# A Mamba-2 block on one core: the order of two matmul groups in TensorE's queue

## The chip, the core and the metric

The kernel runs on one core of a Trainium2 chip. The time is that of the device for one launch, in microseconds. A core has TensorE (matmuls), VectorE, ScalarE, GpSimd and SyncE, each with an instruction queue of its own that is worked off in order; they meet at semaphores. TensorE writes to PSUM only, eight banks of 128 partitions by 512 float32.

## The reference

Input x is 4 batches of 512 tokens by 512 features. All is float32.

```
mod = silu(c) @ wmod                              # shift, scale, gate for both halves
h   = layernorm(x) * (1 + ca) + sa
xBC, z, A_log = split(h @ in_proj_w.T)            # 2048, 1024 and 64 columns
xBC = silu(causal depthwise conv1d(xBC, 4 taps) + bias)
X, B, C = split(xBC)                              # 64 heads of 16; B and C: 8 groups of 64
dt  = softplus(A_log)
y   = chunked state space scan(X, -dt, B, C) + D * X / dt
x   = x + ga * ((y * silu(z + z_bias)) @ out_proj_w.T)
h   = layernorm(x) * (1 + cb) + sb
x   = x + gb * (h @ binarize(w_ffn).T + b_ffn)
```

The scan, for each head and each chunk of tokens, is the sum of a diagonal part, (C B^T masked by the decays inside the chunk) times X, and an off-diagonal part, C times the state that the chunks before have left, scaled by the decay. The state of a chunk is B^T times X weighted by the decay to the chunk's end.

## The kernel before

There are three parts: a first one (layer norm, modulation, weights split in a high and a low half), the main part (input projection, convolution, scan), and a tail (output projection, second layer norm, the last linear layer). The change is in the main part.

The main part goes over 16 steps, a step being one of four pairs of B/C groups (16 heads) and one of four batches. A step has four units of 128 tokens (`U_TOK`), two chunks of 64 each. That makes `NU` = 64 units. The loop runs `v` from -2 to 63, with four slots `sl` in each turn, and every engine has a copy of this loop with its own order of calls. In one turn TensorE runs for unit `v` the scan's matmuls, and prepares later ones:

- slot 0: `offdiagonal(v)` (L1241), `states(v + 1)` (L1254), `gram(v + 1)` (L1280), `diagonal(v)` (L1266);
- slot 1: `turn_x(v + 2)` (transposes of X, L1218);
- slots 2 and 3: `decay(v + 2, 0)` and `(v + 2, 1)` (L1209), and in slot 3 `turn_b(v + 2)` (L1227);
- in nearly all slots `project` (L1200), half a tile of the input projection: 6 matmuls of 128*128 by 512 columns; in some turns `weights` (L1297), two transposes of the next weights; and at the end matmuls of the tail (L1968).

`gram` makes C B^T of a unit, four matmuls of 64 rows by 64 columns of the array (64*64), into columns 384 to 447 of the two PSUM banks named `pair` (`YS`). `diagonal` is 32 matmuls of 64*32, into columns 0 to 127 of the same banks. `offdiagonal` (64*64, columns 128 to 255) and `states` (64*64, columns 256 to 383) write there too. In the trace each of these float32 matmuls has two records: 8 for `gram`, 64 for `diagonal`, 16 for `offdiagonal`, 8 for `states` (half of these two in some units). A matmul that is marked as the last of a group raises the group's semaphore: `g_done`, `yd_done`, `yo_done`, `st_done`.

Other engines on these groups:

- ScalarE writes the exponentials M of a unit (`exponent`, L1373, slots 2 and 3, waits for `yd_done` two units back), X transposed (`spread`, L1381), B transposed (`copy_b`, L1386, raises `bt_read`).
- VectorE, slot 1: `update(v + 1, 0)` adds a chunk's state (L1514, L1517), after `st_done`, `yd_done` and `g_done`; `collect(v)` reads `offdiagonal` and `diagonal` (L1500, L1502), after `yd_done`, `yo_done` and `g_done` of the next unit. Slot 2: `update(v + 1, 1)`, then `mix(v + 1, q)` (L1484) multiplies M by gram's result, after `exp_done` and `g_done`, and raises `m_done`, two for each unit. Convolution taps (L1454) and silu products (L1475) fill the queue between.
- GpSimd weighs X by the decays (`weigh`, L1587), fades the state (L1597), and builds the gated output (L1608, L1622); L1629 makes the low halves of weights.

Of the kernel before, what the change touches and what calls it, by code (L numbers as in the profile page):

```python
# [58 lines left out]
def wait(eng, sem, count):  # L59

    if not isinstance(count, int) or count > 0:
        eng.wait_ge(sem, count)
# [886 lines left out]
def piece_at(slot):  # L949

    gp, r = slot // 64, slot % 64
    if r == 0 and gp > 0:
        return (gp - 1) * 12 + 11
    if r in W_AT and gp < GP - 1:
        return gp * 12 + W_AT[r]
    j = (slot - 4 * OUT_UNIT - 3) // 4 * 2 + (slot % 4 == 0)
    if slot >= 4 * OUT_UNIT + 3 and slot % 4 in (3, 0) and j < NWO + NWF:
        return NWP + j
    return None
# [7 lines left out]
def main_part(nc, s, outer, start, x, w_in, w_out, w_ffn, b_ffn):  # L967

    with ExitStack() as ctx:
# [3 lines left out]
        def sem(name):  # L973
            return outer.enter_context(nc.semaphore("m_" + name))
# [22 lines left out]
        d_done, exp_done, xt_done, xp_done, xw_done, bt_done, bt_read, g_done, m_done = (  # L997
            sem(n) for n in ("d_done", "exp_done", "xt_done", "xp_done", "xw_done", "bt_done", "bt_read", "g_done", "m_done"))
# [16 lines left out]
        def chunk(u, c):  # L1015
            first = (u % UPS) * U_TOK + c * Q
            return slice(first, first + Q)
# [26 lines left out]
        def n_new(u, c):  # L1044

            return (u // UPS) * (NC - 1) + min(2 * (u % UPS) + c + 1, NC - 1)
# [135 lines left out]
        def tensor(pe, tail):  # L1182
            def project(k, part):

                n, t = TILES[k]
                if part == 0:
                    if n % NB == 0 and n >= NB:

                        pe.wait_ge(w_lo_done, (n // NB - 1) * 12 + 2 * W_ORDER.index(t) + 2)
                    if n < NB:  # L1190

                        pe.wait_ge(start.w_pool, start.weights_ready(t))
                        start.wait_low(pe, 4 * n + 3)
                    if k < 3:
                        pe.wait_ge(start.h_act, 5 + k)
                        pe.wait_ge(start.w_act, (4, 8, 12)[k])
                    wait(pe, silu_done, k - 2)
                for m in range(6 * part, 6 * part + 6):
                    kc, w, h = m // 3, (s.w_hi, s.w_hi, s.w_lo)[m % 3], (s.h_hi, s.h_lo, s.h_hi)[m % 3]
                    ins = pe.matmul(A[k % 3][:, :], w[:, t, kc, :], h[:, n % NB, kc, :], start=(m == 0), stop=(m == 11))  # L1200
                if part == 1:
                    ins.then_inc(in_done, 1)

            def decay(u, q):

                if q == 0:
                    pe.wait_ge(rl_ready[u % 2], 64 * (u // 2 + 1))
                wait(pe, exp_done, 2 * u + q)
                pe.matmul(DB[:, :], s.Lm[:, u % 2, q, :], s.R[:, u % 2, q, :], start=True, stop=True).then_inc(d_done, 1)  # L1209
# [11 lines left out]
            def turn_b(u):  # L1221

                n = u // UPS
                if u % UPS == 0:
                    pe.wait_ge(silu_done, TILE_NO[n, 2] + 1)
                wait(pe, bt_read, u)
                pe.transpose(GB[:, 0:P], Bt[:, n % 2, tok(u)], s.ident[:, :]).then_inc(bt_done, 1)  # L1227

            def offdiagonal(u):

                n = u // UPS
                wait(pe, y1_done, u)
                pe.wait_ge(s_new, n_new(u, 1))
                pe.wait_ge(m_done, 2 * u + 2)
                for c in range(2):
                    if u % UPS == 0 and c == 0:
                        continue
                    for j in range(2):
                        for q in range(2):
                            group, strip = slice(64 * q, 64 * q + 64), slice(64 * j, 64 * j + 64)  # L1240
                            ins = pe.matmul(YS[strip, q, P + Q * c:P + Q * c + Q], S[group, (2 * u + c - 1) % 4, strip],  # L1241
                                            Ct[group, n % 2, chunk(u, c)], start=True, stop=True)
                ins.then_inc(yo_done, 1)

            def states(u):

                if u > 0:
                    pe.wait_ge(s_new, n_new(u - 1, 1))
                pe.wait_ge(xw_done, u + 1)
                pe.wait_ge(bt_read, u + 1)  # L1250
                for q in range(2):
                    for c in range(2 if u % UPS < UPS - 1 else 1):
                        half, group = slice(64 * c, 64 * c + 64), slice(64 * q, 64 * q + 64)
                        ins = pe.matmul(YS[group, c, 256:384], BTs[half, group], Xw[half, q, :], start=True, stop=True)  # L1254
                ins.then_inc(st_done, 1)

            def diagonal(u):

                pe.wait_ge(m_done, 2 * u + 2)
                pe.wait_ge(xp_done, u + 1)  # L1260
                for q in range(2):
                    for e in range(2):
                        for j in range(4):
                            for c in range(2):
                                half, h = slice(64 * c, 64 * c + 64), 2 * j + e
                                ins = pe.matmul(YS[32 * j:32 * j + 32, c, q * Q:(q + 1) * Q], Xp[half, u % 2, HG * q + h, :],  # L1266
                                                M[half, u % 2, q, h * Q:(h + 1) * Q], start=(e == 0), stop=(e == 1))
                ins.then_inc(yd_done, 1)

            def gram(u):  # L1270

                n = u // UPS
                if u % UPS == 0:
                    pe.wait_ge(silu_done, TILE_NO[n, 3] + 1)
                pe.wait_ge(bt_read, u + 1)
                wait(pe, m_done, 2 * u)
                for c in range(2):
                    for q in range(2):
                        group = slice(64 * q, 64 * q + 64)
                        ins = pe.matmul(YS[64 * c:64 * c + 64, q, 384:384 + Q], Bt[group, n % 2, chunk(u, c)],  # L1280
                                        Ct[group, n % 2, chunk(u, c)], start=True, stop=True)
                ins.then_inc(g_done, 1)
# [26 lines left out]
            for v in range(-2, NU):  # L1309
                u = v + 2  # L1310
                for sl in range(4):
                    slot = 4 * v + sl
                    if (v, sl) == (-2, 2):
                        start.turn_sections(pe)
                    if (v, sl) == (-1, 0):
                        start.dt_inputs(pe, 1, 1)
                        start.gate_turn(pe)
                    if sl == 0:
                        if v >= 0:
                            offdiagonal(v)  # L1320
                        if 0 <= v + 1 < NU:
                            states(v + 1)
                        if 0 <= v + 1 < NU:
                            gram(v + 1)
                        if v >= 0:
                            diagonal(v)
                    if sl == 2 and u < NU:
                        decay(u, 0)
                    if sl == 3 and u < NU:
                        decay(u, 1)  # L1330
                    if slot + 8 in PART_AT:
                        project(*PART_AT[slot + 8])
                    if sl == 1 and u < NU:
                        if slot >= 1 and piece_at(slot - 1) is not None:
                            pe.wait_ge(w_copied, piece_at(slot - 1) + 1)
                        if v in (-2, 5):
                            pe.wait_ge(start.we_ev, UPS if v < 0 else 2 * UPS)
                        turn_x(u)
                    if sl == 3 and u < NU:
                        turn_b(u)  # L1340
                    if v >= 0 and piece_at(slot) is not None:
                        if sl == 3:
                            pe.wait_ge(xp_done, u + 1)
                        weights(piece_at(slot))
                    if (v, sl) == (4, 3):
                        pe.wait_ge(xp_done, u + 1)
                        start.end_turn(pe, 1)
                    if slot in TAIL_AT:
                        tail.project(pe, *TAIL_AT[slot])
                    if (v, sl) == (NU - 1, 1):  # L1350
                        alpha()
# [696 lines left out]
```

## Time and profile before

| | |
|---|---|
| median of 3 runs | 698.25 us (697.37 to 699.26) |
| the profiled execution | 698.25 us, its span 696.5 us |
| TensorE clock granted, mean | 0.966 of full |
| matmuls / weight loads busy | 637.1 / 499.8 us |
| VectorE / ScalarE / GpSimd busy | 519.6 / 383.4 / 356.2 us |

The span is the time from the first to the last instruction in the trace. "PE" is TensorE's matmuls, "PEld" its weight loads, "DVE" VectorE, "ACT" ScalarE, "POOL" GpSimd, "SP" SyncE; L1280 is line 1280 of the kernel. Matmuls are pipelined: one record lasts longer than the distance to the next start, so distances between starts tell more than durations. A tile shape such as 64*32 is the rows and columns of the array that a matmul uses. A "q" behind an engine's name means its sequencer.

### The profile page before, as it was taken

How to read it: one execution, taken by the hardware profiler on the slowest of the kernel's cores; microseconds unless marked ns; L12 is line 12 of the kernel's file. 1: busy time of each engine (PE TensorE's matmuls, PEld its weight loads, DVE VectorE, ACT ScalarE, POOL GpSimd, SP SyncE). 2: the span in 40 equal slices, each digit the busy share in tenths (PEclk: the TensorE clock that was granted, in tenths of full speed). 3: DMA queues.
4: the chain of work that ended last, by engine and by line, in shares of the span. 5: the costliest groups of instructions: out<-in, count | busy, mean ns of one | idle time of the engine just before them, and what ended most of it. 6: DMA issues, size and time to landing. Idle time of an engine off the chain costs nothing.

```text
span 696.5 us, 21359 instructions
## 1 busy us (share of the span) xinstructions
PE 637.1 (91%) x8371; PEld 499.8 (72%) x8371; DVE 519.6 (75%) x947; ACT 383.4 (55%) x834; POOL 356.2 (51%) x416
## 2 busy tenths in 40 slices
PE   4576987999999999999999999999997899999995
PEld 1463665777777777777777777878775667888884
DVE  6559749997787787867778678777779556786766
ACT  3647532554655545564645565555665525666555
POOL 4546310244754634655445375363754747667652
PEclk9679878999999999999999999999999999999999
DMA  8644202052322222232123142422212664354411
GB/s 280 158 147 136 80 4 75 11 165 76 111 64 87 68 66 70 75 118 69 36 82 111 40 140 83 142 79 74 81 51 81 207 208 122 121 145 145 135 46 61
DMA packets 61914, 70.52 MB, mean 101 GB/s; under 512 B 13972, under 2 KB 33460, under 8 KB 61816
## 3 DMA queue, kind: packets, MB, share of 16 engines
q1 hardware_dynamic: 61816, 69.17, 31.4%
q8 instruction: 67, 1.10, 0.7%
q14 instruction: 31, 0.25, 0.1%
HBM read 54.45 MB, written 14.70 MB: 99 GB/s over the span
## 4 chain that ended last, share of the span: by engine, by line
PE 71%; DVE 13%; issue 5%; POOL 4%; ACT 4%; DMA 1%; SPq 0%; DVEq 0%; POOLq 0%; ACTq 0%
PE bank L1200 32%; PE bank L1968 11%; PE pair L1266 6%; PE bank L1209 4%; PE bank L2001 3%; PE pair L1254 3%; DVE m_cv L1454 2%; PE pair L1241 2%; PE bank L1297 2%; PE bank L1218 2%; DVE chain L600 2%; DVE m_M L1484 1%; PE pair L769 1%; DVE chain L593 1%; DMA h_lo_place<-y_scratch 1%
## 5 line engine op out<-in xcount | busy, mean ns | idle before, releaser
L1454 DVE SCALAR_TENSOR_TENSOR m_cv<-bank,gpc,m_cv 128x511 f32<-128x511 f32 (+2 forms) x192 | 143.3, 747 | 35.5 <-ACT m_cv L1361 30.9
L1200 PE MATMUL bank<-h_hi,w_hi 128*128 128x512 f32 x384 | 160.4, 418 | 2.9 <-POOL h_lo L428 1.5
L1200 PE MATMUL bank<-h_lo,w_hi 128*128 128x512 f32 x384 | 153.0, 399 | 0.0
L1200 PE MATMUL bank<-h_hi,w_lo 128*128 128x512 f32 x384 | 153.0, 398 | 0.0
L1597 POOL TENSOR_TENSOR m_S<-m_S,m_cd 128x128 f32<-128x128 f32 x96 | 39.9, 415 | 160.8 <-DVE m_S L1517 85.4
L1361 ACT ACTIVATE m_cv<-bank,gpc 128x512 f32<-128x512 f32 x96 | 72.0, 750 | 76.7 <-PE bank L1200 75.7
L1200 PEld LDWEIGHTS bank<-h_hi,w_hi 128*128 128x128 f32 x384 | 74.1, 193 | 21.3 <-issue 4.7
L1200 PEld LDWEIGHTS bank<-h_hi,w_lo 128*128 128x128 f32 x384 | 73.4, 191 | 16.9
L1200 PEld LDWEIGHTS bank<-h_lo,w_hi 128*128 128x128 f32 x384 | 74.0, 193 | 14.1
L1373 ACT ACTIVATE m_M<-bank 128x512 f32<-128x512 f32 x128 | 76.2, 595 | 12.7 <-PE bank L1209 11.2
L1484 DVE TENSOR_TENSOR m_M<-m_M,pair 128x512 f32<-128x512 f32 x128 | 81.7, 679 | 0.2 <-issue 0.2
L1587 POOL TENSOR_TENSOR m_Xw<-m_Xp,wend 128x256 f32<-128x256 f32 x64 | 39.9, 623 | 73.8 <-ACT m_Xp L1381 73.8
L1368 ACT ACTIVATE bank<-m_cv 128x512 f32<-128x512 f32 x96 | 58.1, 605 | 3.4 <-DVE m_cv L1454 3.4
L1209 PE MATMUL bank<-R,Lm 84*128 84x512 f32 x128 | 58.2, 454 | 1.8 <-ACT m_M L1373 1.8
L1822 POOL TENSOR_TENSOR t_y_lo<-h_lo_place,t_y_hi 128x1024 fp32r<-128x1024 f32 x16 | 39.1, 2444 | 39.6 <-ACT t_y_hi L1768 35.1
L1266 PE MATMUL pair<-m_M,m_Xp 64*32 64x64 f32 x4096 | 55.5, 225 | 0.2 <-issue 0.2
L1475 DVE SCALAR_TENSOR_TENSOR m_gate<-bank,m_cv 128x512 f32<-128x512 f32 x32 | 22.1, 690 | 42.1 <-ACT bank L1368 42.1
L1968 PE MATMUL bank<-h_hi,t_y_hi 128*128 128x512 f32 x128 | 51.5, 403 | 1.3 <-POOL t_y_lo L1822 1.3
L1968 PE MATMUL bank<-h_hi,t_y_lo 128*128 128x512 f32 x128 | 50.7, 396 | 0.0
L1968 PE MATMUL bank<-h_lo,t_y_hi 128*128 128x512 f32 x128 | 50.7, 396 | 0.0
L1381 ACT ACTIVATE m_Xp<-bank 128x256 f32<-128x256 f32 x64 | 24.3, 380 | 46.3 <-PE bank L1218 46.3
L1266 PEld LDWEIGHTS pair<-m_M,m_Xp 64*32 64x32 f32 x4096 | 44.9, 106 | 4.7 <-issue 0.3
(184 smaller groups left out, 1280.9 us busy)
## 6 DMA issues: line engine op xcount, KB each, us to landing
m_ea<-ea_scratch SPq DMA_DIRECT2D x32, 256.0 KB
m_dd<-dd_scratch SPq DMA_DIRECT2D x32, 256.0 KB
y_scratch<-m_t SPq DMA_DIRECT2D x16, 512.0 KB, 3.5
h_lo_place<-y_scratch SPq DMA_DIRECT2D x16, 512.0 KB, 4.4
p_wm<-in_L_wmod_dram SPq DMA_DIRECT2D x6, 1024.0 KB, 7.5
m_wraw<-in_L_attn_in_proj_w_dram SPq DMA_DIRECT2D x18, 256.0 KB, 3.1
w_lo_place<-in_L_attn_input__dram SPq DMA_DIRECT2D x16, 256.0 KB, 4.7
out_dram<-t_o SPq DMA_DIRECT2D x16, 256.0 KB, 2.3
```

Of the source, the lines that this page charges most:

```text
L1200: ins = pe.matmul(A[k % 3][:, :], w[:, t, kc, :], h[:, n % NB, kc, :], start=(m == 0), stop=(m == 11))
L1209: pe.matmul(DB[:, :], s.Lm[:, u % 2, q, :], s.R[:, u % 2, q, :], start=True, stop=True).then_inc(d_done, 1)
L1266: ins = pe.matmul(YS[32 * j:32 * j + 32, c, q * Q:(q + 1) * Q], Xp[half, u % 2, HG * q + h, :], M[half, u % 2, q, h * Q:(h + 1) * Q], star ...
L1361: act.activation(cv[:, k % 3, :], A[k % 3][:, :], ACT.Identity, scale=scale, bias=bias).then_inc(lin_done, 1)
L1368: act.activation(A[k % 3][:, :], cv[:, k % 3, :], ACT.Tanh).then_inc(tanh_done, 1)
L1373: act.activation(M[:, u % 2, q, :], DB[:, :], ACT.Exp).then_inc(exp_done, 1)
L1454: ins = dve.scalar_tensor_tensor(out=cv[:, k % 3, lag:], in0=A[k % 3][:, 0:L - lag], scalar=s.gpc[:, gp, o:o + 1], in1=cv[:, k % 3, lag:], ...
L1484: dve.tensor_tensor(m, m, g, ALU.mult).then_inc(m_done, 1)
L1587: pool.tensor_tensor(Xw[:, :, :].rearrange("p q (j e d) -> p (q j) e d", e=2, d=HD), src, w, ALU.mult).then_inc(xw_done, 1)
L1597: pool.tensor_tensor(S1[:, c, :].rearrange("p (h d) -> p h d", h=HG), S[:, (m - 1) % 4, :].rearrange("p (h d) -> p h d", h=HG), cd[:, b // ...
L1822: pool.tensor_tensor(y_lo[:, st.b % 2, :, :], yt_v(st.b), y_hi[:, st.b % 2, :, :].bitcast(F32), ALU.subtract).then_inc(ylo_done, 1)
L1968: ins = pe.matmul(OB[i][:, :], y[:, i, k, :], w[k], start=(k == 0 and m == 0), stop=(k == KI - 1 and m == 2))
```

## The change

In `gram` a wait goes: the one on `m_done` for count 2u. In TensorE's loop, slot 0, `diagonal(v)` moves from behind `gram(v + 1)` to before it. TensorE's order in slot 0 becomes `offdiagonal(v)`, `states(v + 1)`, `diagonal(v)`, `gram(v + 1)`. The waits of the other engines stay as they are.

```diff
@@ -1273,7 +1273,6 @@
                 if u % UPS == 0:
                     pe.wait_ge(silu_done, TILE_NO[n, 3] + 1)
                 pe.wait_ge(bt_read, u + 1)
-                wait(pe, m_done, 2 * u)
                 for c in range(2):
                     for q in range(2):
                         group = slice(64 * q, 64 * q + 64)
@@ -1320,10 +1319,10 @@
                             offdiagonal(v)
                         if 0 <= v + 1 < NU:
                             states(v + 1)
+                        if v >= 0:
+                            diagonal(v)
                         if 0 <= v + 1 < NU:
                             gram(v + 1)
-                        if v >= 0:
-                            diagonal(v)
                     if sl == 2 and u < NU:
                         decay(u, 0)
                     if sl == 3 and u < NU:
```

## Rows read from the trace of the kernel before

**Rows 1.** Busy us, share of the span and instructions of each engine.
```profile
PE 637.1 (91%) x8371; PEld 499.8 (72%) x8371; DVE 519.6 (75%) x947; ACT 383.4 (55%) x834; POOL 356.2 (51%) x416
```

**Rows 2.** Busy us of each engine by stretch (start:end, length), then clock, DMA share, GB/s.
```profile
100.00:136.00 36.00, 30.22 (x437) 23.38 (x438) 34.57 (x57) 15.56 (x32) 6.98 (x12) 0.86 0.13 43
...
157.00:507.00 350.00, 346.41 (x5865) 275.04 (x5868) 268.09 (x516) 197.52 (x434) 181.54 (x239) 1.00 0.26 83
507.00:551.00 44.00, 36.94 (x643) 28.48 (x630) 34.95 (x72) 25.68 (x60) 27.64 (x35) 0.96 0.35 110
```

**Rows 3.** The chain of waits by line, 157 to 507 us, then 507 to 551.
```profile
by line: PE bank L1200 56.3%; PE pair L1266 10.5%; PE bank L1209 6.3%; PE pair L1254 5.3%; PE pair L1241 4.2%; PE bank L1297 3.4%; PE bank L1218 2.9%; issue 2.1%; PE pair L1280 1.7%; PE bank L1227 1.5%; DVE m_cv L1454 1.3%; POOL m_t L1622 1
...
by line: PE bank L1200 24.4%; DMA h_lo_place<-y_scratch 15.5%; issue 11.7%; DVE m_cv L1454 6.9%; DVE m_M L1484 4.4%; PE bank L1209 3.4%; PE bank L1297 2.9%; DVE t_wsta L1523 2.8%; DVE t_att L1528 2.8%; SPq L1080 2.6%; DVE m_S L1517 2.0%; PE
```

**Rows 4.** The chain in order of time, pieces of L1266: start us, length us.
```profile
135.67 0.79 PE pair L1266 x53
...
558.31 0.79 PE pair L1266 x53
```

**Rows 5.** Gram's matmuls, 157 to 507 us: ns min/median/max, first and last start.
```profile
L1280 PE MATMUL pair<-m_Ct,m_Bt x400: 216/218/267, 157.4 to 506.3; 64*64 64x64 f32 x134
```

**Rows 6.** Groups by line, whole span: busy us, mean ns, idle before.
```profile
L1280 PE MATMUL pair<-m_Ct,m_Bt 64*64 64x64 f32 x512 | 22.6, 223 | 0.0
```

**Rows 7.** Semaphore instructions of the wait helper on TensorE, 200 to 500 us.
```profile
L62 PEldq EVENT_SEMAPHORE  x157: 51/51/51, 200.4 to 498.9; - x157
```

**Rows 8.** TensorE matmuls in order, 305.9 to 308.5 us: start us, length us.
```profile
306.09 0.38 PE L1297 MATMUL bank<-ident,m_wraw 128*128 128x128 f32 x2
306.40 0.46 PE L1241 MATMUL pair<-m_Ct,m_S 64*64 64x64 f32 x16
306.71 0.45 PE L1254 MATMUL pair<-m_Xw,m_BTs 64*64 64x128 f32 x8
306.95 0.32 PE L1280 MATMUL pair<-m_Ct,m_Bt 64*64 64x64 f32 x8
307.20 0.87 PE L1266 MATMUL pair<-m_M,m_Xp 64*32 64x64 f32 x64
308.00 0.44 PE L1297 MATMUL bank<-ident,m_wraw 128*128 128x128 f32 x2
```

**Rows 9.** The same unit by line: duration ns min/median/max of one matmul.
```profile
L1254 PE MATMUL pair<-m_Xw,m_BTs x8: 269/280/320, 306.7 to 306.9; 64*64 64x128 f32 x8
L1280 PE MATMUL pair<-m_Ct,m_Bt x8: 216/217/218, 306.9 to 307.1; 64*64 64x64 f32 x8
L1266 PE MATMUL pair<-m_M,m_Xp x64: 213/216/240, 307.2 to 307.9; 64*32 64x64 f32 x64
L1297 PE MATMUL bank<-ident,m_wraw x4: 271/272/328, 306.1 to 308.2; 128*128 128x128 f32 x4
```

**Rows 10.** Weight loads in order, 305.9 to 308.5 us.
```profile
307.20 0.70 PEld L1266 LDWEIGHTS pair<-m_M,m_Xp 64*32 64x32 f32 x64
```

**Rows 11.** TensorE matmuls that start before 306.53 us.
```profile
306.40 0.34 PE L1241 MATMUL pair<-m_Ct,m_S 64*64 64x64 f32 x8
```

**Rows 12.** The chain of waits in order, 226 to 238 us.
```profile
234.00 1.30 POOL m_t L1622
...
235.98 0.45 PE pair L1254 x8
```

**Rows 13.** All engines in order, 300 to 308 us: `mix`.
```profile
304.44 1.27 DVE L1484 TENSOR_TENSOR m_M<-m_M,pair 128x512 f32<-128x512 f32 x2
```

**Rows 14.** Who waited for whom, whole span: us in total, times, longest us.
```profile
PE pair L1241 <- DVE m_M L1484: 7.2, 5, 3.4
DVE m_S L1517 <- PE pair L1266: 6.9, 2, 5.6
DVE m_S L1514 <- PE pair L1280: 4.9, 1, 4.9
```

## The prediction

> **What bounds the kernel now.** I read the busy table first: TensorE is at 91% of the span, VectorE at 75%, ScalarE at 55%, GpSimd at 51% [rows 1]. Cut into stretches [rows 2], the units around the change (one unit is 128 tokens of one head group pair, 64 in all) fall into three parts. From 157 to 507 us TensorE is busy 346.41 of 350.00 us at the full granted clock, VectorE only 268.09. From 100 to 136 us it is the other way round: VectorE 34.57 of 36.00, TensorE 30.22. From 507 to 551 us neither is full. Then the chain of waits says what an added TensorE instruction would move. Between 157 and 507 us it is made of matmul groups (L1200 alone 56.3%), "issue" is 2.1% [rows 3]; between 507 and 551 us a DMA landing has 15.5%, and between 100 and 136 us VectorE's load leaves little to TensorE. The `diagonal` call of a unit (L1266) is a piece of this chain of 0.79 us. With a `gram` ahead of it such a piece stands there 50 times, first at 135.67 and last at 558.31 us [rows 4], and 47 of the 50 lie between 157 and 507 us, where there are 50 units (400 gram matmul records, 8 a unit) [rows 5]. So of the 63 units in which `gram` and `diagonal` both run, 50 have them on the chain and 13 have not.
>
> **The change, part by part.** No instruction is added, no size or buffer is changed, and SP's and GpSimd's queues are not touched. Two edits: a wait less, and an exchange of two neighbours in TensorE's queue.
>
> The wait. `gram(v+1)` waits for 2v+2 of `m_done`, which `offdiagonal(v)`, first in the same slot, has waited for with the same number. It is always satisfied. TensorE has no idle time before L1280 [rows 6]. What it costs is at most its semaphore instruction, 51 ns each [rows 7]. In the trace it lies beside the matmuls of `states`: from the last start of these to the first gram matmul it is 0.06 us (below), of which a 128 column matmul needs some 0.05 itself. I take 0; the bounds are 0 and 63 x 0.051 = 3.2 us of gain.
>
> The exchange. It costs what it does to the seams between groups of different tile shape, so I take the seams from one unit [rows 8], at full clock. A line's last start is its start plus its length less one matmul's duration [rows 9] (L1241's is L1280's, of the same shape and columns): L1297 starts last at 306.20 (306.09 + 0.38 - 0.27), L1241 at 306.64, L1254 at 306.89, L1280 at 307.05, L1266 at 307.85. Start to start across the seams:
> - L1297 (128*128, 128 columns, 272 ns) to L1241 (64*64): 0.20 us.
> - L1241 to L1254 and L1254 to L1280, same tile shape: 0.07 and 0.06 us.
> - L1280 (64*64, 218 ns) to L1266 (64*32): 0.15 us.
> - L1266 (64*32, 216 ns) to L1297 (128*128): 0.15 us.
> So at each of the three changes of shape the next group starts about 0.07 us before the last matmul of the former one ends, whatever it is (272 less 70 is 0.20; 218 and 216 less 70 are 0.15), and its weight loads start no earlier: L1266's first at 307.20, with its first matmul [rows 10]. Within a group of one shape new starts follow closely: 16 of L1241 in 0.24 us.
>
> Before, the queue runs states, gram, diagonal, next, with three changes of shape in a unit. After, it runs states (64*64), diagonal (64*32), gram (64*64), next (128*128): four. From the last start of states to the first of the next group:
> - before: 0.06, gram's own starts 0.10 (306.95 to 307.05), 0.15, diagonal's 0.64, 0.15: 1.10 us.
> - after: states to diagonal 0.20 (its matmuls have 128 columns and last 269 to 280 ns, as L1297's), diagonal's 0.64, diagonal to gram 0.15, gram's own starts 0.13, gram to next 0.15: 1.27 us.
> Gram's 0.13 is that of the first eight matmuls of `offdiagonal`, which have its shape and follow a change of shape: with the window cut at 306.53 us they are x8 and 0.34 us long, less 0.22 [rows 11]. The difference is 0.16 us a unit (0.162 with the rows' nanoseconds).
>
> Two of these seams no row shows. For 64*32 to 64*64 the nearest rows are the two with 64*32 on one side (0.15); the far end is the seam without a change of shape (0.06), at which gram would also run in 0.10: then the unit costs 0.20 - 0.15 + 0.06 - 0.06 = 0.05 us more. States to diagonal lies between 0.15 and 0.20.
>
> On the chain stand 50 such units: 50 x 0.162 = 8.1 us. The 13 others have a cover. In the early ones VectorE is the bound. Three in the middle lie beside a detour over GpSimd, of which the one at 229 us is shown: the chain comes through GpSimd's L1622 to states at 235.98 [rows 12]. Between 507 and 551 us it is the DMA and VectorE [rows 3]. If all cover were gone it would be 63 x 0.162 = 10.2 us. I add 0.4 for units where the cover is thinner than 0.16, and take 8.5 us.
>
> Who waits for the two groups. `yd_done` now comes after 0.20 + 0.64 instead of 0.06 + 0.10 + 0.15 + 0.64, so 0.11 us earlier. `update(v+1, 0)` and `collect(v)` on VectorE need `g_done` as well, and it comes 0.16 us later than `yd_done` came, still just before the next group, as before. Behind them in VectorE's queue stand `mix`, the convolution taps and the silu products; they have room: `mix` ends at 305.71 (304.44 + 1.27), `offdiagonal`, which needs it, starts at 306.40, 0.69 us later [rows 8, 13]. On ScalarE `exponent` and `spread` wait for `yd_done`, but in slot 2, where these groups are long past. VectorE's waits for the two groups are small: 6.9 us after L1266, 4.9 after L1280 in the whole span [rows 14].
>
> The rule of the Trainium skill that speaks against the change is in TensorEngine Tiling (Array Packing), section Tiling Modes: a change of the tiling mode, and not of the tile alone, drains the engine. The rows show it at the three seams of today, 0.15 to 0.20 us against 0.06; that it holds for 64*32 back to 64*64 no row shows, and by the rule the sum stays as it is.
>
> **Rivals.**
> A. No drain back to 64*64: both shapes have 64 rows, and gram's weights get in beside the last diagonal matmuls. For it: within a shape loads do run ahead. Against: at the seam 64*64 to 64*32, the same pair, they did not [rows 10]. Then 0.05 us x 50 = 2.5 us more, with the cover 2 to 3.5: about 701.
> On this the Trainium skill has a sentence in TensorE: Matmul & The Clock Gate, Part 3, The mechanism: a weight load that targets a row group without conflict, or the background buffer, is pulled ahead of matmuls in flight. By it gram's four loads would be hidden; at none of today's changes of shape does the trace agree.
> B. Faster: the seams cost nothing net and the queue is shorter by the removed instruction. Its place is the seam in front of gram, its price 63 x 0.051 = 3.2 us less, so 695.0. It decides if the drain does not depend on the number of shape changes. Against it: the idle time of 0.0 before L1280, and a seam of 0.06 that a matmul fills.
> C. Dearer: VectorE gets `g_done` late in units where it has no room, `mix` ends late, and `offdiagonal` stands. It decides where the 0.69 us above has shrunk to under 0.16. TensorE waits for L1484 only 7.2 us in 5 places now [rows 14]. If the covered units pay as well, the 10.2 us above come, and with 1 us of such waits 11: 708.5 to 709.5.
>
> **How the numbers follow.** The profiled execution took 698.25 us, span 696.5 and 1.75 around it, and it is also the median of the runs; so the sum is made against 698.25. 698.25 + 8.5 = 706.7. Chances: forecast 0.70 (its own range 705.3 to 708.2), C 0.12, A 0.12, B 0.06. The range of 8 in 10 leaves out B, the cheap side of A and the far end of C: 702.3 to 709.3. A measurement of this kernel tells about 0.3% (2.1 us) from no change: faster 0.05, same 0.06 (the low end of A and a small B), slower 0.89.
>
> **What would show it.** In the changed profile: between L1266's last start and L1280's first some 0.15 us, and the same from L1280 to the next 128*128 group; L1254 to L1266 0.20. In a stretch where TensorE is full the units lie 0.16 us further apart; those 50 units take 358.1 us instead of 350. TensorE's busy sum hardly falls as a share. VectorE's waits for L1266 pass to L1280. The forecast is wrong if L1280 starts within 0.07 us of L1266's last start, or if the seams are as said and the span grew by less than 5 us: then TensorE had room that its chain does not show.

## The result and the profile after

The changed kernel takes 705.57 us (703.74 to 705.88, 4 runs) against 697.81 us before (4 runs): ratio 1.0108, 95% interval 1.0077 to 1.0141, so 7.8 us slower, and by the interval 5.4 to 9.8. Forecast were 8.5 us and 706.7.

The profiled execution has a span of 702.7 us in 704.39. The first line is that of busy times, the second the windows of 157 to 507 us in the columns of [rows 2]:

```profile
PE 643.8 (92%) x8371; PEld 497.9 (71%) x8371; DVE 522.5 (74%) x947; ACT 383.5 (55%) x834; POOL 355.9 (51%) x416
...
157.00:507.00 350.00, 346.45 (x5671) 269.10 (x5670) 264.88 (x506) 193.38 (x424) 179.99 (x238) 1.00 0.26 82
```

The busy times cannot show the loss: in this window TensorE is busy for the same 346.4 us as in [rows 2]. But it has only 5671 matmul records in it where it had 5865. It does less work in the same busy time: at a change of shape a record of 0.22 us lasts longer than the 0.15 us to the next start, so the lost time does not show as idle. The count overstates the loss, as the window's edges cut different pieces of a unit in the two traces: 194 records are 3.3%, and the time of 48 units below grew by 2.0%.

The seams show it. This is TensorE's order in one unit of the changed kernel, start and length in us; it answers to [rows 8]:

```profile
379.83 0.46 PE L1241 MATMUL pair<-m_Ct,m_S 64*64 64x64 f32 x16
380.36 0.45 PE L1254 MATMUL pair<-m_Xw,m_BTs 64*64 64x128 f32 x8
380.74 0.86 PE L1266 MATMUL pair<-m_M,m_Xp 64*32 64x64 f32 x64
381.53 0.34 PE L1279 MATMUL pair<-m_Ct,m_Bt 64*64 64x64 f32 x8
381.81 0.50 PE L1200 MATMUL bank<-h_hi,w_hi 128*128 128x512 f32 x1
```

States starts last at 380.54 (380.36 + 0.45 - 0.27) and diagonal at 380.74: 0.20. Diagonal starts last at 381.38 and gram (L1279) at 381.53: 0.15. Gram's own starts take 0.34 - 0.22 = 0.12, and the projection follows 0.15 or 0.16 later. From the last start of states to the projection it is 1.27 us; before it was 1.10 or 1.11. It is no matter of one unit: in the 46 units between 157 and 495 us the three distances are 0.20, 0.14 to 0.17 and 0.15. The weight loads again start with the matmuls (2 or 3 ns ahead), not among those of the former group:

```profile
380.74 0.70 PEld L1266 LDWEIGHTS pair<-m_M,m_Xp 64*32 64x32 f32 x64 [0.17 <-issue]
381.53 0.21 PEld L1279 LDWEIGHTS pair<-m_Ct,m_Bt 64*64 64x64 f32 x8
```

For a length that can be compared between kernels I take the start of `turn_b` (L1227), of which there is one a unit, and count 48 units from the ninth. Before (first two rows) and after (last two), start us and length:

```profile
163.58 0.27 PE L1227 MATMUL bank<-ident,m_Bt 128*128 128x128 f32 x1
...
505.19 0.27 PE L1227 MATMUL bank<-ident,m_Bt 128*128 128x128 f32 x1
```

```profile
162.18 0.27 PE L1227 MATMUL bank<-ident,m_Bt 128*128 128x128 f32 x1
...
510.78 0.27 PE L1227 MATMUL bank<-ident,m_Bt 128*128 128x128 f32 x1
```

The 48 units took 341.61 us and take 348.60 us: 6.99 more, 0.146 a unit. The eight units ahead of them take 70.8 us where they took 70.1, the ones behind the same 50.5. So nearly all of the loss lies where TensorE is full. The 0.7 us in the eight units ahead is too small to read anything from it: in e2 below, as fast as before, the units behind the stretch alone took 51.9 us. The profiled spans differ by only 6.2 us, because in this execution the main part began 2.1 us earlier (first `turn_b` at 91.36 us, before 93.46); the part ahead of it does not have the change in it.

Who waits now: VectorE's waits for the slot's last group went to L1279; they answer to [rows 14] and to the first line here, which is of the kernel before. They are small still.

```profile
DVE m_S L1514 <- PE pair L1266: 2.0, 5, 0.5
```

```profile
DVE m_S L1516 <- PE pair L1279: 8.6, 8, 5.6
DVE m_S L1513 <- PE pair L1279: 7.9, 6, 4.5
PE pair L1241 <- DVE m_M L1483: 7.6, 5, 3.4
```

### The profile page after: what moved, and what is told of

Same layout as the page of the kernel before. It is cut to its first block, busy times and chain, and to the rows that moved or that the text cites. A ratio compares the mean times of both kernels' runs of the same rounds, so it can differ in the third digit from the quotient of the medians.

```text
span 702.7 us, 21311 instructions
## 1 busy us (share of the span) xinstructions
PE 643.8 (92%) x8371; PEld 497.9 (71%) x8371; DVE 522.5 (74%) x947; ACT 383.5 (55%) x834; POOL 355.9 (51%) x416
## 4 chain that ended last, share of the span: by engine, by line
PE 71%; DVE 11%; issue 5%; ACT 4%; POOL 4%; DMA 3%; SPq 2%; POOLq 0%; DVEq 0%; ACTq 0%
PE bank L1200 31%; PE bank L1967 11%; PE pair L1266 6%; PE bank L1209 4%; PE bank L2000 3%; PE pair L1254 3%; PE pair L1241 2%; PE bank L1296 2%; PE pair L1279 2%; DVE m_cv L1453 2%; PE bank L1218 2%; DVE chain L600 2%; DMA p_wa_raw<-in_L_attn_in_proj_w_dram 2%; DVE chain L593 1%; PE pair L769 1%
## 5 line engine op out<-in xcount | busy, mean ns | idle before, releaser
L1266 PE MATMUL pair<-m_M,m_Xp 64*32 64x64 f32 x4096 | 56.1, 227 | 0.6 <-issue 0.6
L1266 PEld LDWEIGHTS pair<-m_M,m_Xp 64*32 64x32 f32 x4096 | 45.6, 106 | 11.9 <-issue 11.8
```

## The experiments

e1 to e7 were timed beside the kernel before, whose medians were 697.84 us (e1 to e4) and 696.85 us (e5 to e7, on another chip); each ratio is to the median beside it. The row of the changed kernel is that of the result above. "48 units" is the length between the same two `turn_b` starts, in one profiled execution of each kernel. A "half diag" is one half of `diagonal`.

| kernel | slot 0 on TensorE | shape changes a unit | median us | ratio, interval | 48 units, us |
|---|---|---|---|---|---|
| before | off, states, gram, diag | 3 | 697.8 | | 341.61 |
| after | off, states, diag, gram | 4 | 705.57 | 1.0108 (1.0077 to 1.0141) | 348.60 |
| e1 | as after, wait kept | 4 | 705.26 | 1.0107 (1.0085 to 1.0129) | 348.96 |
| e2 | as before, wait removed | 3 | 698.11 | 1.0000 (0.9983 to 1.0018) | 341.57 |
| e3 | as after, gram in 64*32 | 3 | 704.57 | 1.0098 (1.0074 to 1.0122) | 344.51 |
| e4 | off, states, half diag, gram, half diag | 5 | 705.65 | 1.0111 (1.0088 to 1.0135) | 347.85 |
| e5 | diag, off, states, gram | 3 | 689.61 | 0.9889 (0.9861 to 0.9918) | 333.23 |
| e6 | off, diag, states, gram | 4 | 695.33 | 0.9972 (0.9952 to 0.9992) | 337.38 |
| e7 | half diag, off, states, gram, half diag | 4 | 688.10 | 0.9880 (0.9848 to 0.9912) | 331.17 |

**e1, the exchange alone.** The kernel before, with the two calls exchanged and the wait kept.

> The exchange alone, the wait on m_done kept. Theory (seams between tile shapes: a fourth change of shape per unit costs 0.16 us on a full TensorE): as the changed kernel, ratio to before 1.011, 705.6 us, within 1 us of it. Rival (the removed wait gives part of it back): 1 to 3 us above the changed kernel, 706.5 to 708.5.

It took 705.26 us, the changed kernel's time. The exchange is the whole effect.

**e2, the wait alone.**

```diff
-                wait(pe, m_done, 2 * u)
```

> The wait on m_done removed, the old order kept. Theory: no change, 697.8 us within 0.7. Rival (the semaphore instruction of 51 ns is on the path): 3.2 us faster, 694.6.

Ratio 1.0000, and 341.57 us for the 48 units against 341.61. A wait that is always satisfied, and whose semaphore instruction runs while matmuls still start, costs nothing here.

**e3, gram in diagonal's shape.** The changed kernel, with

```diff
-                for c in range(2):
-                    for q in range(2):
-                        group = slice(64 * q, 64 * q + 64)
-                        ins = pe.matmul(YS[64 * c:64 * c + 64, q, 384:384 + Q], Bt[group, n % 2, chunk(u, c)],
+                for r in range(2):
+                    for c in range(2):
+                        for q in range(2):
+                            group, rows = slice(64 * q, 64 * q + 64), slice(64 * c + 32 * r, 64 * c + 32 * r + 32)
+                            ins = pe.matmul(YS[rows, q, 384:384 + Q], Bt[group, n % 2, half_chunk(u, c, r)],
```

> The changed kernel, with gram built from 8 matmuls of 64*32 in place of 4 of 64*64, so diagonal, gram have one tile shape and a unit has three changes of shape as before, but TensorE has more matmuls. Theory: the seam from diagonal to gram falls from 0.15 to under 0.03 us, gram's own starts grow from 0.13 to about 0.17, so 0.08 us less a unit, 4 us less than the changed kernel: 701.5 us (700 to 703). Rival (the cost is g_done coming last and VectorE being late by it): g_done still comes last in the slot, so it stays at 705 us or more.

The median missed: 704.57 us, not 701.5. The stretch that the theory speaks of did what was expected, 344.51 us, 4.1 less than the changed kernel. A unit of it, TensorE in order (L1270 is diagonal, L1284 gram):

```profile
389.83 0.80 PE L1270 MATMUL pair<-m_M,m_Xp 64*32 64x64 f32 x60
390.41 0.24 PE L1284 MATMUL pair<-m_Ct,m_Bt 64*32 64x64 f32 x1
390.42 0.22 PE L1270 MATMUL pair<-m_M,m_Xp 64*32 64x64 f32 x1
390.43 0.24 PE L1284 MATMUL pair<-m_Ct,m_Bt 64*32 64x64 f32 x1
390.44 0.25 PE L1270 MATMUL pair<-m_M,m_Xp 64*32 64x64 f32 x3
390.49 0.38 PE L1284 MATMUL pair<-m_Ct,m_Bt 64*32 64x64 f32 x14
390.80 0.50 PE L1204 MATMUL bank<-h_hi,w_hi 128*128 128x512 f32 x1
```

There is no seam left between the two groups: gram's first matmul even starts among diagonal's last, and `g_done` is still raised last. From diagonal's first start to the projection it is 0.97 us; in the changed kernel it is 1.07 (380.74 to 381.81). The rival, a late `g_done`, has no room for this gain, though the median by itself looks like its forecast. What spoiled the time lies earlier: the eight units before the stretch take 74.5 us instead of 70.8, and TensorE stands in the middle of gram. (The profiled execution took 702.35 us, the shortest of the six; so the profile explains the missing gain, not each run's time.) First the waits of TensorE between 95 and 170 us (us in total, times, longest), then the longest but one, in order:

```profile
PE pair L1284 <- issue: 5.0, 4, 2.0
```

```profile
127.92 0.34 PE L1284 MATMUL pair<-m_Ct,m_Bt 64*32 64x64 f32 x11
130.06 0.30 PE L1284 MATMUL pair<-m_Ct,m_Bt 64*32 64x64 f32 x3 [1.80 <-issue]
```

Between the two rows the instructions are of one call with no wait in it. The kernel has 512 more matmul records and as many weight loads. That the instructions came late is one reading: the DMA view has packets of the instruction queues (11 between 95 and 170 us), and each of the four stands begins 0.2 to 2.0 us after one of them starts. But every kernel here has the same 11 packets in that stretch, and the others do not stand so. No run tests it; the cause stays open.

**e4, diagonal cut in two around gram.** `diagonal(v, 0)`, `gram(v + 1)`, `diagonal(v, 1)`, each half one of its two `q`; nothing else.

> The changed kernel, with diagonal cut in two halves of 16 matmuls and gram between them: states, half, gram, half. No instruction more, five changes of tile shape a unit in place of four. Theory: 0.15 us a unit more on 48 to 50 units, 7 us above the changed kernel: 713 us (711.5 to 714.5). Rival (the cost is that g_done comes last): gram is again ahead of diagonal's end, so the time falls back towards 698 to 701 us.

Both forecasts were wrong: 705.65 us, the changed kernel's own time; the 48 units took 0.75 us less with one seam more each. The unit (L1267 is diagonal, L1281 gram):

```profile
388.36 0.44 PE L1254 MATMUL pair<-m_Xw,m_BTs 64*64 64x128 f32 x4
388.73 0.45 PE L1267 MATMUL pair<-m_M,m_Xp 64*32 64x64 f32 x32
389.11 0.34 PE L1281 MATMUL pair<-m_Ct,m_Bt 64*64 64x64 f32 x8
389.39 0.45 PE L1267 MATMUL pair<-m_M,m_Xp 64*32 64x64 f32 x32
389.77 0.50 PE L1200 MATMUL bank<-h_hi,w_hi 128*128 128x512 f32 x1
```

The seams are all there and of the expected size: 388.96 to 389.11 and 389.24 to 389.39, 0.15 each. But the starts of a half take only 0.45 - 0.22 = 0.23 us (0.238 in the trace's nanoseconds, in every unit from 157 to 495 us), and two of them 0.48, while the whole diagonal takes 0.64. In the kernel before, too, the first 32 starts are quick: cut at 307.46 us the row of L1266 is

```profile
307.20 0.45 PE L1266 MATMUL pair<-m_M,m_Xp 64*32 64x64 f32 x32
```

0.24 us for 32 starts, about 8 ns each, and 0.40 for the other 32, about 13 ns each. In the second half 0.08 us pass between the 32nd start and the 34th; cut at 307.52 us the row still has only 33 starts:

```profile
307.20 0.48 PE L1266 MATMUL pair<-m_M,m_Xp 64*32 64x64 f32 x33
```

After that they come at 11 ns on average. Cutting the diagonal added a seam of 0.15 us and took away 0.17.

Why the second half is slow is a reading, not shown. 32 matmul records with their 32 weight loads are 64 records; so I read the seam as time in which the queue in front of TensorE fills, and the first 32 matmuls behind it as that queue running out. A queue of 64 for TensorE is what the Trainium skill states in TensorE: Matmul & The Clock Gate (its table of specifications); the place of the step fits that number. e3 fits too: there the 14 starts of gram behind the whole diagonal take 0.16 us, 12 ns each, the slow pace in another group. But the 32nd record is also where `diagonal` goes from `q` = 0 to `q` = 1, in every kernel here, and e4 and e7 cut it just there. That the change of `q` without a pause is what costs is a rival that no run tests; a cut after 16 records would tell.

The next three kernels tell a seam that is repaid from a count of seams alone, and try an order that follows from the trace. In units without a weights piece `states` stands for `bt_read`, which ScalarE raises: from L1241's last start (380.07 above) to L1254's first (380.36) it is 0.29 us, where [rows 8] has 0.07. In the changed kernel ScalarE's copy ends at 380.22, 0.14 us ahead of states, and this 0.14 is the same in nearly every unit there (in e5, with the diagonal between, it is 0.68 or more):

```profile
379.94 0.28 ACT L1385 ACTIVATE m_BTs<-bank 128x128 f32<-128x128 f32 x1 [0.44 <-PE bank L1227]
```

**e5, diagonal first.** The kernel before, with `diagonal(v)` ahead of `offdiagonal(v)`; the waits on `y1_done`, `s_new` and `m_done` go from `offdiagonal` into `diagonal`, and the one in `gram` goes.

```diff
+                            diagonal(v)
                             offdiagonal(v)
                         if 0 <= v + 1 < NU:
                             states(v + 1)
                         if 0 <= v + 1 < NU:
                             gram(v + 1)
-                        if v >= 0:
-                            diagonal(v)
```

> The kernel before with diagonal moved to the front of the slot (diagonal, offdiagonal, states, gram) and the waits that offdiagonal made for it moved along. Three changes of tile shape a unit, as before. Theory (seams count, and states now waits for bt_read in the shadow of diagonal): the 0.22 us in front of states in the units that have no weights piece goes, some 33 of 63 units, and nothing is added: 7 us less than before, 691 us (689.5 to 693). Rival (diagonal ahead of gram is itself what costs, as VectorE gets g_done last): 703 to 706 us, as the changed kernel.

689.61 us, 7.2 below the kernel before. The unit (L1265 diagonal, L1238 offdiagonal, L1251 states, L1278 gram):

```profile
384.46 0.86 PE L1265 MATMUL pair<-m_M,m_Xp 64*32 64x64 f32 x64
385.25 0.46 PE L1238 MATMUL pair<-m_Ct,m_S 64*64 64x64 f32 x16
385.53 0.40 PE L1251 MATMUL pair<-m_Xw,m_BTs 64*64 64x128 f32 x8
385.75 0.29 PE L1278 MATMUL pair<-m_Ct,m_Bt 64*64 64x64 f32 x8
385.98 0.50 PE L1200 MATMUL bank<-h_hi,w_hi 128*128 128x512 f32 x1
```

Offdiagonal starts last at 385.49, states at 385.53: of the 0.29 us 0.04 are left. Most units without a weights piece are 0.23 to 0.34 us shorter, somewhat more than the 0.22 expected, as states and gram also start closer together. VectorE gets `g_done` last in the slot here as in the changed kernel, and the time is 7.2 us below the kernel before: a late `g_done` is not what made the changed kernel slow.

**e6, diagonal second.** The same calls, `offdiagonal`, `diagonal`, `states`, `gram`.

> Order offdiagonal, diagonal, states, gram: the same instructions as the run before it, four changes of tile shape in place of three, and states again in diagonal's shadow. Theory: one seam more, 0.15 us less the 0.07 of the seam inside a shape and plus 0.02 for the fresh start, so 0.10 us a unit, 5 to 6 us above diagonal first: 696.5 us (695 to 698). Rival (a seam is always repaid by the queue that fills meanwhile, as the split diagonal suggests): the same time as diagonal first, within 1 us.

695.33 us. Against e5 it has one change of shape more, and 48 units take 4.15 us more, 0.09 a unit (0.10 expected). Here the seam is not repaid. By the reading above it has nothing to repay: the diagonal comes whole and behind a seam in both orders, and the group ahead of it has 16 records.

**e7, halves around the rest.** As e5, with `diagonal(v, 1)` behind `gram(v + 1)`.

> Diagonal first, but its second half of 16 matmuls moved behind gram: half, offdiagonal, states, gram, half. Four changes of tile shape in place of three. Refill theory (TensorE issues the first 32 records of a diagonal in 0.24 us and the other 32 in 0.40, because the queue ahead of it has run out; a seam lets it fill): a seam of 0.15 is added and 0.17 us of slow issue goes, so the time is that of diagonal first within 1.5 us. Pure seam theory: 0.15 us a unit more, 7 to 9 us above diagonal first.

688.10 us, and 331.17 us for the 48 units, 2.1 less than e5 with one seam more each. Its unit (L1266 diagonal):

```profile
382.19 0.46 PE L1266 MATMUL pair<-m_M,m_Xp 64*32 64x64 f32 x32
382.57 0.46 PE L1238 MATMUL pair<-m_Ct,m_S 64*64 64x64 f32 x16
382.85 0.40 PE L1251 MATMUL pair<-m_Xw,m_BTs 64*64 64x128 f32 x8
383.07 0.29 PE L1280 MATMUL pair<-m_Ct,m_Bt 64*64 64x64 f32 x8
383.30 0.46 PE L1266 MATMUL pair<-m_M,m_Xp 64*32 64x64 f32 x32
383.68 0.50 PE L1200 MATMUL bank<-h_hi,w_hi 128*128 128x512 f32 x1
```

A theory that counts seams alone wanted 7 to 9 us more than e5, and is out. The refill theory's own forecast, within 1.5 us of e5, held by the medians (1.5 us). The intervals of e5 and e7 overlap, so that e7 is the faster rests on the 48 units of one profile each, and a seam of 0.15 against 0.17 us gives only some 0.9 of these 2.1 us. Both are faster than the kernel before by intervals that leave out 1, though by little more than 1%.

## Why the prediction was right

**Where TensorE is full the change falls on the path.** Right: 6.99 us lie in the 48 units at full clock, of 7.8 by the medians. Where the rest lies one profile of each kernel cannot tell.

**The wait costs nothing.** Right, shown by e2 (ratio 1.0000) and by e1, which has it and is as slow.

**The seams.** Right in each term: 0.20, 0.15, 0.15 us and 0.12 to 0.13 for gram. The seam from 64*32 back to 64*64, which no row of before showed, is 0.15, as its neighbours are. The rule of the Trainium skill in TensorEngine Tiling (Array Packing), Tiling Modes, that a change of mode drains the engine, holds in the trace for every direction seen here, with 0.15 to 0.20 us each. Rival A, no drain between shapes with the same rows, is refuted: no weight load came early at any change of shape. e3 shows the opposite case, one shape and no seam at all.

**0.162 us a unit, and how many units pay.** The size of one unit is right: the median over the 48 is 0.159 us more. How many pay was put too high. 6.99 us over 48 units are 0.146, because some units pay next to nothing. Five of them are clear; the pitch of one is 7.33 us before (227.69 to 235.02) and 7.35 after (227.84 to 235.19). In each of the five the group behind slot 0 starts 0.16 us later, as elsewhere, and the time comes back in slot 3, where TensorE's weight loads pause ahead of a projection, for 0.31 to 0.38 us in the kernel before. Two of these pauses before, then the first of them after:

```profile
233.53 0.19 PEld L1200 LDWEIGHTS bank<-h_hi,w_hi 128*128 128x128 f32 x1 [0.38 <-POOL w_lo L1629]
489.20 0.19 PEld L1200 LDWEIGHTS bank<-h_hi,w_hi 128*128 128x128 f32 x1 [0.31 <-DVE m_xs L1475]
```

```profile
233.68 0.19 PEld L1200 LDWEIGHTS bank<-h_hi,w_hi 128*128 128x128 f32 x1 [0.18 <-POOL w_lo L1628]
```

Here the projection started 0.38 us after the matmul ahead of it (233.18 to 233.56) and starts 0.24 us after it now (233.53 to 233.77). Three of the five (233.53, 347.08, 460.58) are the units of the detours over GpSimd [rows 12], which the prediction had left out of its count. The two others (176.44, 489.20) it had as payers, because the chain of waits runs through TensorE there; a pause of the weight loads that a chain piece hides can still take up 0.16 us. Besides, two pairs of neighbours (from 284.09 and from 397.65 us) pay 0.12 and 0.15 us, once for two. There such a pause (0.16 and 0.29) goes too, but other starts move as well, and what covers them is not shown. So the prediction had 45 payers among these 48 units, 7.3 us, and there were 41, for which 41 x 0.162 is 6.6. The 0.4 us added for thinner cover elsewhere has no counterpart either. More of the 0.7 us by which the forecast lay too high cannot be accounted for: by the interval above, 8.5 and 7.8 us cannot be told apart.

**VectorE has room.** Right. The waits of its state updates for the two groups are 16.5 us in all against 13.8 (the 11.8 in [rows 14] and 2.0 more of L1514 after L1266), but TensorE's waits for `mix` are 7.6 against 7.2. Rival C did not come. e5 shows it by itself: `g_done` last in the slot, and faster by 7.2 us. Rival B (695.0) did not come either.

**What the prediction had no term for.** It priced a seam as pure loss. That holds for the seam it was asked about: the diagonal is run from one end to the other in both kernels, with its 0.64 us unchanged, so there was nothing to win back. That the change asked for was of this kind is luck, as the prediction did not ask whether a seam can be repaid. e4 and e7 show that one in the middle of the diagonal is. Had the change been e4, the same reasoning would have said 713 us, as I did, and been 7 us off.

## What to carry to other kernels

Count the changes of tile shape in TensorE's order, read start to start and not from busy times: each cost the last matmul's duration less about 0.07 us here, at the full clock, so keep groups of one shape together. Put the group whose inputs have long been there in front of the one that waits for a result just being made: that gave 7 us here, about as much as the bad order cost. Before counting a seam as a loss, look in the trace whether the group it cuts starts its later matmuls more slowly than its first ones. And when counting the units that will pay, look at the pauses of the weight loads too, and not at the chain of waits alone.

## What the runs showed of the hardware

- A run of 64 small matmul records (64*32, 64 columns) behind a change of shape starts its first 32 at 8 ns and the rest at 13 ns each, of which 0.08 us are one pause at the 33rd. Two runs of 32 with a seam between them are as quick as one of 64, or quicker: 348.60 us with the diagonal whole and 347.85 cut for 48 units, and 333.23 and 331.17. Whether a queue that runs out is the cause, or the change of `q` at the same place, stays open.
- With the same tile shape the matmul records of two groups interleave in their starts (e3), although one group stands wholly ahead of the other in the program.
- 5.0 us of stalls inside one group of matmuls with no wait, in four places between 95 and 170 us (e3), in a program with 512 more matmul records. Of the other traces only that of the changed kernel has anything like it in that stretch, once and for 0.58 us, inside the six matmuls of a projection (up to 108.97 us). Their cause stays open.
